# A new order of expert blocks in a transformer layer: five dense blocks last, with the final normalisation in eight sections beside them

## What is computed

```python
x = layernorm(x + attention(x))     # 16 heads of 8
x = layernorm(x + experts(x))
# experts:
S = sigmoid(xt @ Wg).T              # 8 experts x 4096 tokens
G, I = top_k(S, 1024)               # each expert picks 1024 tokens
ex = xt[I]
hid = gelu(einsum('ekh,ehf->ekf', ex, W1) + b1)        # 128 -> 512
out = (einsum('ekf,efh->ekh', hid, W2) + b2) * G[..., None]
new_x = zeros_like(xt).at[I.reshape(-1)].add(out)
```

## Time and profile before

| what | us |
|---|---|
| median of 3 runs (lowest, highest) | 536.09 (535.33, 537.52) |
| the profiled execution's own time | 533.78 |
| its span, first to last instruction | 532.2 |
| busy in the span: PE, DVE, ACT, POOL | 469.9, 330.3, 295.3, 266.3 |
| last PE instruction ends | 505.3 |

### The profile page before, as it was taken

The page is one execution under the profiler, slowest core; times in us unless marked ns, Lnnn a source line. Parts: engine busy times, 40 slices in busy tenths (PEclk is TensorE's granted clock), DMA queues, the critical chain, the costliest instruction groups (busy, mean ns, idle before and its releaser), DMA issues.

```text
span 532.2 us, 10902 instructions
## 1 busy us (share of the span) xinstructions
PE 469.9 (88%) x3910; PEld 384.9 (72%) x3911; DVE 330.3 (62%) x874; ACT 295.3 (55%) x587; POOL 266.3 (50%) x360
## 2 busy tenths in 40 slices
PE   5999999989999999999985788899999979999900
PEld 4777777767777777777763577789999969999900
DVE  5577776766767667677775797873223533444284
ACT  3277777757777677766763352354554433444325
POOL 9460534326333353531236400684787878786461
PEclk9999999999999999999999699899999988999965
DMA  3422233474433333233021100012333324232445
GB/s 90 79 67 55 52 76 87 112 167 71 92 87 70 73 73 77 58 82 83 23 61 43 40 16 7 24 47 56 86 57 64 43 47 62 48 35 26 85 101 156
DMA packets 47709, 35.65 MB, mean 67 GB/s; under 512 B 5704, under 2 KB 42600, under 8 KB 47656
## 3 DMA queue, kind: packets, MB, share of 16 engines
q1 hardware_dynamic: 39656, 28.18, 22.4%
q0 software_dynamic: 7552, 6.49, 8.2%
q10 hardware_dynamic: 448, 0.28, 0.3%
HBM read 12.46 MB, written 9.57 MB: 41 GB/s over the span
## 4 chain that ended last, share of the span: by engine, by line
PE 75%; DVE 11%; DMA 5%; ACT 3%; issue 2%; POOL 2%; SPq 1%; ACTq 0%; POOLq 0%; DVEq 0%
PE banks L1200 16%; PE banks L1137 12%; PE banks L1120 11%; PE banks L1100 10%; PE banks L1187 4%; PE banks L1189 4%; PE banks L1188 4%; PE banks L1051 3%; PE banks L1029 2%; DVE v_stage L1500 2%; PE banks L1075 1%; PE banks L1061 1%; PE banks L1067 1%; DVE probs L1563 1%; PE banks L1163 1%
## 5 line engine op out<-in xcount | busy, mean ns | idle before, releaser
L1347 DVE TENSOR_REDUCE row_max<-banks 128x2 f32<-128x512 f32 x256 | 166.2, 680 | 54.5 <-PE banks L1100 53.7
L891 ACT ACTIVATE probs<-banks 128x512 f32<-128x512 f32 x256 | 140.8, 595 | 28.6 <-PE banks L1120 26.9
L943 ACT ACTIVATE hT_flat<-banks,b_cols 128x512 f32<-128x512 f32 x112 | 76.7, 688 | 102.6 <-PE banks L1189 101.4
L1100 PE MATMUL banks<-k_pad,q_stack 96*128 96x256 f32 x512 | 118.3, 315 | 1.2 <-DMA k_pad<-k_lo 1.2
L1120 PE MATMUL banks<-q_stack,k_pad 100*128 100x256 f32 (+3 forms) x512 | 106.4, 289 | 5.3 <-ACT probs L891 2.1
L1200 PE MATMUL banks<-w_buf,hT_flat 128*128 128x128 f32 x896 | 108.5, 280 | 0.0
L1200 PEld LDWEIGHTS banks<-w_buf,hT_flat 128*128 128x128 f32 x896 | 106.7, 196 | 1.4
L1100 PEld LDWEIGHTS banks<-k_pad,q_stack 96*128 96x128 f32 x512 | 82.2, 197 | 9.0 <-issue 6.5
L1120 PEld LDWEIGHTS banks<-q_stack,k_pad 100*128 100x128 f32 (+3 forms) x512 | 78.8, 190 | 11.3 <-issue 7.9
L788 POOL DMA_INDIRECT summed<-v_flat,index x40 | 65.4, 1635 | 15.2 <-issue 11.3
L1137 PE MATMUL banks<-probs,v_flat 128*32 128x256 f32 x1024 | 68.5, 385 | 0.7 <-ACT probs L891 0.7
(11 more groups left out here) (230 smaller groups left out, 656.8 us busy)
## 6 DMA issues: line engine op xcount, KB each, us to landing
q_stack<-q_hi SPq DMA_DIRECT2D x32, 128.0 KB, 3.3
w_buf<-in_L_ffn_W SPq DMA_DIRECT2D x16, 256.0 KB, 3.0
k_pad<-k_hi SPq DMA_DIRECT2D x60, 64.0 KB
x_table<-rows SPq DMA_DIRECT2D x16, 136.0 KB, 2.4
rows<-in_L_attn_x SPq DMA_DIRECT2D x8, 256.0 KB, 3.1
q_stack<-q_lo SPq DMA_DIRECT2D x16, 128.0 KB, 3.4
summed<-rows SPq DMA_DIRECT2D x16, 128.0 KB, 2.8
probs<-summed SPq DMA_DIRECT2D x4, 512.0 KB, 6.0
```

The costliest lines, as they stand in the source:

```text
L891: s.activation(probs[:, h % 8], ps_second[:, h % 2], ACT.Exp, scale=SCALE).then_inc(exp_done, 1)
L943: s.activation(hT[:, i % 2, f], banks[:, up_bank(i, f)], ACT.Gelu, bias=b1_cols[:, FBLK * e + f:FBLK * e + f + 1]).then_inc(gelu_done, 1)
L1100: mm = t_.matmul(ps_first[:, h % 3, i * SEQ:(i + 1) * SEQ], q_stack[0:ROWS_1, n % 2, side, t, i * P:(i + 1) * P], k_pad[0:ROWS_1, n % 2, c ...
L1347: v.tensor_reduce(row_max[:, c, 2 * t:2 * t + 2], ps_first[:, h % 3].rearrange("p (i j) -> p i j", i=2), AX, ALU.max).then_inc(first_free, 1)
```

## The change

- `ORDER` is new. The blocks of expert 1 stand right behind those of expert 0. From expert 2 on each sparse pair is followed by one dense block, and d7.3 to d7.7 stand at the end.
- `down_first`: behind the second half of a sparse expert, down is issued before up of the next block. One up pair (s0.1) moves into the search, by `pieces(... else 1)`.
- `summed` and the table of gathered rows are stored partition by partition (`(p t)` in place of `(t p)`), and the token numbers follow (`token_i`). A section's load then reads 2 KB in a piece, where a quarter's read 512 B.
- The last stage works in eight sections of four tiles. The square root moves from ACT and DVE to POOL, as a power of -0.5 (`root_section`). DVE scales 4, 2, 1, 1, 1, 1, 1 and 2 tiles of the sections, ACT the rest. DVE takes the statistics of sections 0 and 1 before d7.6 is added, those of 2 to 4 before d7.7.
- `gate_first` gets new places in DVE's order, and some semaphores of the start are merged, with the same waits.

```diff
+ORDER = ([("d", 6, c) for c in range(6)] + [("s", 0, 0), ("s", 0, 1), ("s", 1, 0), ("s", 1, 1), ("d", 6, 6), ("d", 6, 7),
+         ("s", 2, 0), ("s", 2, 1), ("d", 7, 0), ("s", 3, 0), ("s", 3, 1), ("d", 7, 1), ("s", 4, 0), ("s", 4, 1),
+         ("d", 7, 2), ("s", 5, 0), ("s", 5, 1)] + [("d", 7, c) for c in range(3, QUADS)])
...
+def down_first(i):
+    return i > 0 and ORDER[i - 1][0] == "s" and ORDER[i - 1][2] == 1
...
+        elif down_first(i):
+            parts = [downs(i, range(4)), ups(i, range(4))]
...
-        summed_rows = summed.rearrange("(t p) d -> p t d", p=P)
+        summed_rows = summed.rearrange("(p t) d -> p t d", p=P)
+        x1_rows = x1_table.rearrange("(p t) g -> p t g", p=P)
...
+        BY_DVE = (4, 2, 1, 1, 1, 1, 1, 2)
...
+        def load_section(queue, q):
+            queue.dma_start(xc_all[:, q * QT:(q + 1) * QT], summed_rows[:, q * QT:(q + 1) * QT]).then_inc(f_in[q], 16)
...
+            def add_section(q):
                 pool.wait_ge(f_in[q], 16)
-                pool.wait_ge(dense_done, 2 * q + 2)
+                pool.wait_ge(dense_done, q + 1)
                 passed(pool, pool_waits)
...
+                g.tensor_tensor(xc_all[:, at], xc_all[:, at], rows[:, at, 0:D], ALU.add).then_inc(f_added, 1)
+            def root_section(q):
+                at = slice(QT * q, QT * (q + 1))
+                pool.wait_ge(f_averaged, QT * (q + 1))
+                g.tensor_tensor(f_sd[:, at], f_mv[:, at, 1], eps_pair[:, 0:QT], ALU.add).then_inc(f_rooted, 1)
+                pool.wait_ge(f_rooted, 2 * q + 1)
+                g.tensor_tensor(f_rstd[:, at], f_sd[:, at], minus_half[:, 0:QT], ALU.pow).then_inc(f_rooted, 1)
+            for q in range(SECTIONS):
+                add_section(q)
+                if q:
+                    root_section(q - 1)
+            root_section(SECTIONS - 1)
...
-                s.activation(f_sd[:, q * QT:(q + 1) * QT].unsqueeze(2), f_mv[:, q * QT:(q + 1) * QT, 1:2], ACT.Sqrt,
-                             bias=eps_pair[:, 0:1]).then_inc(f_rooted, 1)
...
-                if part < HOT_PARTS[2] - 1:
-                    pieces(2)
+                pieces(2 if part < HOT_PARTS[2] - 1 else 1)
...
+                    if (i, 3) in TURNS_AT and down_first(i):
+                        copy_taken(TURNS_AT[(i, 3)])
...
-                v.reciprocal(f_rstd[:, part], f_sd[:, part]).then_inc(linked_step, 1)
...
+            blocks(FIRST_SPARSE + 1, end - 2)
             statistics(0)
-            blocks(end - 2, end - 1)
             statistics(1)
             scales(0)
+            blocks(end - 2, end - 1)
+            for q in range(2, 5):
+                statistics(q)
+                scales(q - 1)
             blocks(end - 1, end)
-            statistics(2)
-            scales(1)
-            statistics(3)
-            scales(2)
-            scales(3)
+            for q in range(5, SECTIONS):
+                statistics(q)
+                scales(q - 1)
+            scales(SECTIONS - 1)
```

More of the change, by code:

```diff
@@ L65, with ups, downs @@
 TURN_NUMBER = {block: i for i, block in enumerate([("d", 6, c) for c in range(QUADS)] + SPARSE_BLOCKS)}
+def down_first(i):
+    return i > 0 and ORDER[i - 1][0] == "s" and ORDER[i - 1][2] == 1
 def pieces_of(n):
[L71 to L77, removed]
+    def ups(i, fs):
+        for f in fs if i < n else ():
+            yield "up", (i, f)
+            if (i, f) in TURNS_AT:
+                yield "turn", TURNS_AT[(i, f)]
+    def downs(i, cs):
         for c in cs if i else ():
@@ L82, in pieces_of @@
     for i in range(n + 1):
-        if i < FINE:
-            parts = [((f,), (f,)) for f in range(4)]
+        if i <= FIRST_SPARSE:
+            parts = [ups(i, (0, 1)), downs(i, (0, 1)), ups(i, (2, 3)), downs(i, (2, 3))]
         elif i < PAIRED:
-            parts = [part for at in (0, 2) for part in (((at, at + 1), ()), ((), (at, at + 1)))]
-        else:
-            parts = [(range(4), ()), ((), range(4))]
-        pieces += [list(items(i, fs, cs)) for fs, cs in parts]
+            parts = [ups(i, (0, 1)), downs(i, range(4)), ups(i, (2, 3))]
+        elif down_first(i):
+            parts = [downs(i, range(4)), ups(i, range(4))]
+        else:
+            parts = [ups(i, range(4)), downs(i, range(4))]
+        pieces += [list(part) for part in parts]
     return pieces
@@ L379, in post_ln_layer @@
         f_added = sem("f_added")
-        f_in = [sem(f"f_in{i}") for i in range(4)]
+        f_in = [sem(f"f_in{i}") for i in range(SECTIONS)]
         f_statted, f_averaged, f_rooted = sem("f_statted"), sem("f_averaged"), sem("f_rooted")
@@ L415, in free_down, with by_dve, tiles_by @@
                 engine.wait_ge(dense_read, c + 1)
-        BY_DVE = 2
-        QT = TILES // 4
+        BY_DVE = (4, 2, 1, 1, 1, 1, 1, 2)
+        def by_dve(section):
+            return BY_DVE[section]
+        def tiles_by(engine_is_dve, section):
+            return sum(by_dve(i) if engine_is_dve else QT - by_dve(i) for i in range(section + 1))
+        def load_section(queue, q):
+            queue.dma_start(xc_all[:, q * QT:(q + 1) * QT], summed_rows[:, q * QT:(q + 1) * QT]).then_inc(f_in[q], 16)
         def q_rows(term):
@@ L436, in first_lane @@
             for term in terms:
[L437 removed]
+                queue.wait_ge(first_cut if term == 1 else first_hi_made, 2 * side + 2)
                 queue.dma_start(k_pad[k_rows(term, c), 0, c, :, cols].bitcast(F32),
@@ L1682, in _ @@
             CUT_AT = {AT[("s", 0, 1)]: 2, AT[("d", 6, 6)]: 3, AT[("d", 6, 7)]: 4, AT[("d", 7, 0)]: 5}
-            FIRST_AT = {AT[("d", 7, c)] - 1: c for c in range(QUADS)}
+            FIRST_AT = {AT[block]: c for c, block in enumerate(
+                (("s", 2, 0), ("s", 2, 1), ("d", 7, 0), ("s", 3, 0), ("s", 3, 1), ("d", 7, 1), ("s", 4, 0), ("s", 4, 1)))}
             def blocks(first, last):
                 for i in range(first, last):
-                    if (i, 3) in TURNS_AT:
+                    if (i, 3) in TURNS_AT and not down_first(i):
                         copy_taken(TURNS_AT[(i, 3)])
```

110 lines of the change are left out of this document (51 added, 59 removed), and 3 rows, old and new, of the table ORDER.

## The result

| | median us | runs |
|---|---|---|
| before, same comparison | 536.15 (532.13 to 540.93) | 20 |
| the change | 538.66 (536.29 to 543.83) | 20 |

The ratio is 1.0079, with a 95% interval of 1.0054 to 1.0105. The forecast was 537.2 in a range of 531.5 to 542.0, so the range holds. But by the bound of 0.5% the change is slower, and that class had been given 0.30, against 0.45 for no change. The profiled execution took 537.02, its span 535.3; forecast were 534.9 and 533.3.

What follows compares the result with a forecast made beforehand. POOL was taken to pace the last stage: roots done 528.5, plus 1.0 scaling, 2.9 store and 0.9 for a hit on DVE gave span 533.3, 1.1 us more than before, so median 537.2, range 531.5 to 542.0.

Steps and rivals of the forecast that it cites:

- waits at s4.0: PE at expert 4's first turn: 1.3 us for POOL's gathers, then 1.4 for ACT's copy and DVE's subtraction.
- waits at s5.0: PE at expert 5's first turn: 3.7 us for POOL's gathers, then 1.4 us behind the transposes.
- first root, POOL's wait for it: Last stage: POOL waits 2.9 us, until 508.0, for section 0's statistics, queued on DVE behind block d7.5.
- DVE's hit: Last stage: POOL's additions slow DVE's sum at block d7.5 once, adding 0.9 us to the chain.
- PE and POOL up to the last scatter: Expert stage: PE waits for gathers at experts 4 and 5; expert 5's scatters begin at 482.4 and land at 499.2.
- The clock loss: PE after expert 5's first turn: about six microseconds at half speed lose 3.0 us, charged once.
- The sum is 528.5 + 1.0 + 2.9: End of the program: POOL's last root at 528.5, 1.0 for scaling and gaps, 2.9 for the store: 532.4.
- Who sets the pace of the last stage: Last stage: POOL leads; eight sections of addition and root need 22.3 us, and relieving ACT and DVE saves nothing.
- the second rival: Last stage: DVE and POOL stop each other, six DVE sums lose 0.94 each, 4.7 us more: 541.9; chance 0.18.
- d7.5 in time: Faster rival: dense block d7.5 is done 3 us sooner, POOL runs through from 502.4, time 532.5; chance 0.25.
- The rows that lie badly: Gathers and scatters: rows 32 times as far apart land up to 1.7 us later, twice: 537.2 to 540.6; chance 0.12.
- That PE's end bounds: End of the expert stage: excluded, since block d7.7 is added by 516.9, before POOL comes to it.

Runs made afterwards that it cites:

- d3: The changed kernel with the last stage's root back on ACT and DVE, POOL only adding: ratio to the kernel before 0.9970, span 529.5 us.
- d4: The changed kernel with four dense blocks last and the root on ACT and DVE, run twice: ratios to the kernel before 0.9954 and 0.9983.
- d1: The kernel before plus one tiny POOL memset behind ACT's last tile, read by nobody: ratio 1.0033, span 535.0 us.
- d2: The changed kernel with block d7.3 moved ahead of expert 5, so four dense blocks stand last: ratio to the kernel before 1.0023, span 533.9 us.
- d6: The changed kernel with the old layout of gathered and scattered tables (tile times 128 plus partition): ratio to the kernel before 1.0067, span 538.9 us.
- d8: The changed kernel with the old order of blocks (three dense last), new last stage kept: ratio to the kernel before 1.0063, span 536.9 us.
- d11: The changed kernel with the old order of blocks and the root on ACT and DVE: ratio to the kernel before 1.0000, span 530.4 us.
- d12: The kernel before with only the order of blocks replaced, four dense blocks last: ratio to the kernel before 1.0024, span 534.6 us.
- d13: Four dense blocks last, root on ACT and DVE, ACT scaling more tiles in the first two sections: ratio to the kernel before 0.9894, span 530.1 us.

## Why the prediction was right, and where it was wrong

| step | forecast | measured |
|---|---|---|
| first scatter; gathers of experts 4 and 5 | 367.0; 428.6, 454.0 | 367.3; 428.6, 453.9 |
| waits at s4.0 | 1.3, then 1.4 | 0.93, then 1.45 |
| waits at s5.0 | 3.7, then 1.4 | 3.26, then 1.45 |
| down of d7.5 done | 504.4 | 503.2 |
| first scatter of expert 5 | 482.4 | 481.5 |
| first section there | 502.4 | 501.2 |
| first root, POOL's wait for it | 508.0, 2.9 | 506.7, 2.99 |
| POOL's waits behind that | 0.9, and 0.9 of DVE's hit | 2.55, 1.82, 0.29 |
| POOL's last root done, with the hit | 529.4 | 529.6 |
| ACT's last tile done | 530.4 | 530.7 |
| end of the span | 533.3 | 535.3 |

**PE and POOL up to the last scatter: right.** The stall at s5.0, the granted clock behind it and all places are within 1.3 us. The clock loss was sized too high, 3.0 against about 2.2: the transposes took 1.12 instead of 0.66, and up products followed each other at 0.43 us instead of 0.23 from 462.86 to about 466.4. Part of the slow time fell into the wait of 1.45, where it costs nothing.

**The end: the step that failed.** "The sum is 528.5 + 1.0 + 2.9" took what lay behind ACT's last tile before and carried it over. The 2.9 is right wherever the store is last (d3 and d4 end 2.9 behind ACT). But the change makes POOL work to 529.55, and POOL's queue closes 5.5 us behind its last instruction. The term that was missing is 1.7 us, most of the 2.0 by which the span was missed; d1 shows the mechanism by itself. The rows for it were in the profile of before, with the end of that drain at 526.2. I had not asked what is late next behind an engine that was done early.

**Who sets the pace of the last stage: wrong, and hidden in the sum.** "ACT and DVE lose a square root and a reciprocal of well under a microsecond each, which saves nothing, since POOL sets the pace" has the leader wrong. From 503.31 on the chain lies on DVE, but for the first and the last root, and POOL waits for it: 4.66 us behind the first root, where it was to be busy almost without gaps. I counted one hit of POOL on DVE, 0.9; there are six, 5.7 in all, four of them at a place I had not thought of, the small instruction that follows each root. That is the second rival's mechanism, but only two of the six sums that it named were hit (1.6 us), so it is chance that the amounts nearly agree (5.7 and 5.6). Its time of 541.9 was not reached: POOL's waits behind the first root came out 2.9 above the forecast's 1.8 with the hit, while POOL's own work was 1.4 shorter (an addition takes 1.29 on the mean, not 1.37, and a root 1.27 to 1.37, not 1.42) and the stage began 1.3 sooner. Three errors cancelled, so the forecast of POOL's end is right by 0.2 for the wrong reason.

The Trainium skill, page "SBUF — State Buffer", section "Who interferes with whom", has the rule: a VectorE instruction with two inputs from SBUF contends with a GpSimd instruction that reads SBUF. The traces agree where POOL adds: beside an addition the small instruction went from 0.13 us to between 1.04 and 1.24, and a sum from 0.69 to between 1.06 and 1.65, while the statistics (one input) took 1.64 for eight tiles beside additions before and 0.86 for four in the change. Beside the power the traces do not show it (0.69 at 520.38). I had applied the rule to the sums alone.

**The rivals.** d7.5 in time: d2 shows that case. The first wait goes, 2.9 us, but the stage and the drain stay, so it is no gain over before. The rows that lie badly: d6 shows nothing of it. That PE's end bounds was excluded, rightly as to PE itself (its last product ends near 513), but d7.5 did cost 2.9 as forecast.

**Why the change is slower.** Its last scatter starts 3.4 us earlier. Behind it, five dense blocks cost 2.9 (d2) and the root on POOL costs the rest: by d8 and d11, or d2 and d4, 3.9, of which 1.7 are the drain. That the others are DVE's hits and the waits for POOL is read from the rows and not parted by a run. The sections by themselves give back 0.3 to 0.6 (33.7 to 34.0 against 34.3). 34.3 + 2.9 + 3.9 - 0.5 = 40.6, measured are 40.7. The parts are not independent: the fifth block costs 2.9 with the root on POOL, 1.7 with it on ACT and DVE (33.9 to 35.6) and 5.5 in quarters (34.4 to 39.9). So 6.5 lost and 3.4 gained make the 3.1 of the spans. The 3.4 are the gain of the order together with `down_first` (the table under d12). In the timed runs that gain is bounded only by d11 against d4, whose intervals overlap.

## What to carry to other kernels

Work that is moved onto an engine that used to finish early has a second price at the end of the program: ask when that engine's queue closes, here 5.5 us behind POOL's last instruction, and compare it with the last store. A small root that looks free on POOL is paid on DVE where POOL's next addition stands right behind it: here DVE's instruction that waits for the root then ran beside that addition, four times, and ended with it. Find the instruction that directly follows each moved step, and look at what the other engine starts at that moment. And a cover of dense blocks behind the last gathered ones pays only as long as its results are there when the last stage asks for them: four did that here, the fifth cost 2.9 us.

## What the runs showed of the hardware that was not expected

- POOL's closing drain ended 5.5 us behind POOL's last instruction in all fourteen profiles: behind an addition, a power and a memset of 0.10 us.
- A DVE instruction with two inputs of 128x4 numbers took 0.13 to 0.16 us alone and 1.04 to 1.24 beside POOL's addition of 128x512; in the change it ended 0.02 us behind the addition all four times. Beside POOL's power on 128x4, DVE's sum of 128x512 at 520.38 kept its 0.69.
- DVE's scaling of a 128x128 tile, with one input of that size, is held up too: 3.09 us for four beside POOL's additions, 1.11 without, and 1.36 for a single tile in d13, whose later single tiles took 0.34.
- Gathers and scatters of rows that lie 32 times as far apart for neighbouring partitions were no slower: the stall for gathers was 4.2 us in both layouts, a gather landed in 2.5 and 2.6 us and a scatter in 3.3 in both (medians of the change and of d6).
